# Two groups of value products moved to later steps of the masked slots in a six-layer attention kernel

## The reference, cut to what matters

```python
scores = jnp.einsum('bhqd,bhkd->bhqk', q, k) * scale
scores = scores * smask                       # (i & j) == 0
a = jax.nn.softmax(scores, axis=-1)
att = jnp.einsum('bhqk,bhkd->bhqd', a, v)
att = att.transpose(0, 2, 1, 3).reshape(Bx, Sx, Dx) @ wo + bo_
h = _ln(h + att, g1, be1)
ff = jax.nn.gelu(h @ w1 + b1_, approximate=False) @ w2 + b2_
h = _ln(h + ff, g2, be2)
```

## Time and profile before

| | us |
|---|---|
| median of 3 runs | 1603.87 (1602.07 to 1606.7) |
| the profiled execution, whole | 1600.91 |
| its span, first to last instruction | 1599.1 |
| PE busy | 1290.9 (81%) |
| DVE busy | 934.3 (58%) |
| ACT busy | 892.1 (56%) |
| POOL busy | 353.7 (22%) |

### The profile page before, as it was taken

One profiled execution on the slowest core, in us unless ns is written; L12 is line 12 of the kernel. 1 busy time (PEld: TensorE's weight loads), 2 busy tenths in 40 slices (PEclk: granted clock), 3 DMA queues, 4 the chain that ended last, 5 costly groups with the idle time before them and its releaser, 6 DMA issues.

```text
span 1599.1 us, 63841 instructions
## 1 busy us (share of the span) xinstructions
PE 1290.9 (81%) x28552; PEld 712.7 (45%) x28552; DVE 934.3 (58%) x1953; ACT 892.1 (56%) x1531; POOL 353.7 (22%) x567
## 2 busy tenths in 40 slices
PE   2678899889998989889998899888898887575833
PEld 1345555555555555455555555554343333131311
DVE  3554555555555556554555565545777577686456
ACT  1256666566666666666666666665455654243710
POOL 3122222222222222122222222132111010101021
PEclk7799999999999999999999999999999999798966
DMA  8443344423442443334433433342232221100000
GB/s 162 94 94 91 77 92 93 105 64 70 86 106 75 92 94 87 92 50 93 91 89 91 96 81 80 75 87 73 36 74 56 60 61 25 31 2 4 8 7 7
DMA packets 133895, 114.07 MB, mean 71 GB/s; under 512 B 42368, under 2 KB 121054, under 8 KB 133214
## 3 DMA queue, kind: packets, MB, share of 16 engines
q1 hardware_dynamic: 133622, 109.99, 31.4%
HBM read 62.69 MB, written 47.25 MB: 69 GB/s over the span
## 4 chain that ended last, share of the span: by engine, by line
PE 36%; issue 25%; DVE 22%; POOL 8%; ACT 5%; DMA 3%; SPq 1%; POOLq 0%; DVEq 0%; ACTq 0%
PE pD L711 14%; PE pT L711 7%; DVE MX L1105 7%; PE pV L781 7%; PE pS L728 5%; DVE DEN L1302 4%; PE pD L884 3%; DVE X L1227 2%; POOL RS L1421 2%; ACT PT L1013 2%; DVE R L1318 1%; DVE YE L1219 1%; ACT SQ L1028 1%; DVE CC L1157 1%; POOL VS L1481 1%
## 5 line engine op out<-in xcount | busy, mean ns | idle before, releaser
L1013 ACT ACTIVATE PT<-pT 128x512 f32<-128x512 f32 x1120 | 640.2, 596 | 506.4 <-PE pT L711 496.2
L1105 DVE TENSOR_REDUCE MX<-pS 128x1 f32<-128x512 f32 (+4 forms) x928 | 501.1, 574 | 440.5 <-PE pS L728 434.6
L711 PE MATMUL pT<-Qop,Kop 128*32 128x256 bf16 (+2 forms) x7168 | 454.3, 304 | 30.4 <-ACT PT L1013 20.9
L728 PE MATMUL pS<-Kop,Qop 128*32 128x128 bf16 (+4 forms) x7168 | 317.6, 259 | 86.9 <-DVE MX L1105 53.2
L781 PE MATMUL pV<-PT,Vp 128*32 128x256 f32 (+2 forms) x3584 | 319.8, 439 | 0.9 <-ACT PT L1013 0.7
L728 PEld LDWEIGHTS pS<-Kop,Qop 128*32 128x32 bf16 x7168 | 180.7, 98 | 266.2 <-DVE MX L1105 122.8
L711 PEld LDWEIGHTS pT<-Qop,Kop 128*32 128x32 bf16 x7168 | 186.9, 97 | 188.8 <-issue 87.1
L781 PEld LDWEIGHTS pV<-PT,Vp 128*32 128x32 f32 x3584 | 125.9, 111 | 69.6 <-issue 25.0
L1421 POOL TENSOR_TENSOR RS<-VAR,MHALF 128x4 f32<-128x4 f32 x60 | 60.6, 1011 | 419.4 <-DVE VAR L1164 419.4
L1455 POOL TENSOR_TENSOR ATT<-NUM,DEN 128x512 f32<-128x512 f32 x28 | 35.6, 1272 | 383.8 <-DVE DEN L1302 383.8
L711 PE MATMUL pD<-HIDT,W 128*32 128x512 f32 x768 | 105.5, 597 | 0.0
(11 more groups left out here) (146 smaller groups left out, 1284.2 us busy)
## 6 DMA issues: line engine op xcount, KB each, us to landing
Qop<-Qs SPq DMA_DIRECT2D x56, 384.0 KB
Kop<-Ks SPq DMA_DIRECT2D x56, 384.0 KB
Qs<-XS SPq DMA_DIRECT2D x28, 384.0 KB, 2.6
Ks<-XS SPq DMA_DIRECT2D x28, 384.0 KB, 3.0
Qs<-XS SPq DMA_DIRECT2D x28, 256.0 KB, 3.0
Ks<-XS SPq DMA_DIRECT2D x28, 256.0 KB, 3.0
EM<-Es SPq DMA_DIRECT2D x24, 256.0 KB, 3.2
Ms<-MROW SPq DMA_DIRECT2D x336, 4.0 KB, 1.4
```

The costliest lines, as they stand in the source:

```text
L711: ins = matmul(dst[c:min(c + 32, cols)], lhs[:, c:min(c + 32, cols)], rhs, start=start, stop=stop, tile_position=(0, c))
L728: ins = matmul(pS[32 * c:32 * c + 32, k % 2, at:at + w], Qop[:, it.par, h, R * qb:R * (qb + 1)], Kop[:, it.par, h, :] if qb == 0 or it.ful ...
L1013: ac.activation(dst, pT[:, k % 2, :], ACT.Exp, scale=SCALE).then_inc(t_used, 1)
L1105: ins = ve.tensor_reduce(MX[:, u, g2, qbs[0]:qbs[-1] + 1:step], pS[:, k % 2, at:at + w * len(qbs)].rearrange("p (h n) -> p h n", n=w), axi ...
```

## The change

The first step of group 0's value product in a slot with a masked C goes from 10 to 14, that of group 2 from 29 to 30. Group 1 (steps 23 to 25) and group 3 (0 to 2 of the next slot) stay.

```diff
                     if prev_last and step in ((1,) if Z.full else (0, 1, 2)):
                         value_product(Z, 3, [3] if Z.full else PIECES[step + 1])
-                    for g, first_step in ((0, 10), (1, 23), (2, 29)):
+                    for g, first_step in ((0, 14), (1, 23), (2, 30)):
                         if C is not None and not C.full and step - first_step + 1 in PIECES:
                             value_product(C, g, PIECES[step - first_step + 1])
```

## The result

The changed kernel takes 1625.91 us in the median of 3 runs (1621.4 to 1634.43) against 1603.87 us; the ratio is 1.0144, with a 95% interval of 1.0073 to 1.0214. A second comparison with more executions gave 1624.69 against 1607.2 us, ratio 1.0109 (1.0076 to 1.0142): 17.5 us slower, 12 to 23 us by the interval. Slower was forecast, with 13.2 us.

The account below looks back on a forecast made before the run. PE was taken to bound the kernel, busy 1290.9 of 1599.1 us. Terms 9.3 + 2.9 - 1.4 + 2.4 + 0 + 0 = +13.2 us on the 1603.87 us median gave 1617.1 us, range 1603 to 1628 us.

Parts of the forecast that it names:

- Sequence 0, the order: Group 0 falls behind the bias products' wait, of which 0.39 us is absorbed before VAR0: 6 x 1.55 = +9.3 us.
- Sequence 0, the clock: PE's half clock after the pause lengthened to 5.5 us: 6 x 0.4 = +2.4 us, ends 0 and 5.3.
- Sequences 2 and 3: Tiles 1 to 3 behind XC0 exceed the wait before VAR0, which starts 0.26 us later: 11 x 0.26 = +2.9 us.
- Sequence 1: Earlier R lets XC0 start about 0.7 us earlier, more work before VAR0: 5 x 0.27 = -1.4 us.
- Group 2: Steps 30 to 32: moved tiles just fit the gap before RB1, 0 us; ends 0 and 5.1 us in 23 slots.

Follow-up runs that it names:

- group 0 alone: Kernel before with only group 0's first step moved from 10 to 14, group 2 left at 29: ratio 1.0075, 12.1 us slower.
- group 0 with sequence 0 only: Kernel before with group 0 moved to step 14 only in the six slots whose Z is of sequence 0: ratio 1.0114, 18.3 us slower.
- group 2 alone: Kernel before with only group 2's first step moved from 29 to 30: ratio 1.0025, 4.0 us slower.
- group 0 elsewhere: Kernel before with group 0 moved to step 14 except where Z is of sequence 0: ratio 1.0023, 3.7 us slower.
- the filled pause: Changed kernel, score unit 13 repeated 18 times ahead of the bias products' wait in sequence-0 slots: ratio 1.0041, 6.6 us slower than before.
- the two fastest: Kernel before with sequence-0 bias products behind XC0: 0.9891; the same plus DVE's BQK ahead of DEN and its reciprocal: 0.9884, 1588.72 us.

## Why the prediction was right, and where it was not

- **Sequence 0, the order: right.** 1.55 us a slot was foreseen; the table has 48.42 - 46.96 = 1.46 and 48.47 - 46.86 = 1.61. The pause of 5.5 us, the lost wait before the variance and the place of the loss came as described, and the runs with group 0 in these slots only, and in all but these, put the whole loss there.
- **Sequence 0, the clock: mis-sized.** I had taken 0.4 us a slot, near the low end, since five of six rows showed the short stretch. It cost 0.8 to 1.1 us more, 5 to 7 us in six slots instead of 2.4, near the high end of my bound. The step that failed is the argument from counting. Five of the six rows were slots in which the clock fell with work already running, 0.7 to 1.4 us behind the pause; in the sixth, the long one, it fell inside the pause:

```profile
120.00:121.10 1.10, 0.00 (x0) 0.00 (x0) 0.96 (x2) 0.71 (x2) 1.10 (x2) 1.00 0.58 212
121.20:122.50 1.30, 0.00 (x0) 0.00 (x1) 0.75 (x1) 0.89 (x2) 1.04 (x1) 0.50 0.00 0
307.70:308.80 1.10, 1.10 (x76) 1.10 (x80) 0.11 (x1) 0.00 (x0) 0.00 (x0) 1.00 0.89 303
```

  In the traces with the pause of 5.5 us in the full kernel (after twice, group 0 alone, group 0 with sequence 0 only) the clock fell inside the pause in all 24 slots, and the work at the low level was 3.1 to 6.4 us long. With the pause of 3.76 us it was 3.2 to 3.4 us in 20 slots of 24 (before twice, group 2 alone, group 0 elsewhere) and 5.4 to 6.5 us in the other four. (A fall inside the pause does not suffice: three of the 20 short ones have it too, by 0.1 to 0.2 us.) So the longer pause makes the dear case common; the filled pause shows that it is the pause. But the size varies by trace: behind the same pause of 5.5 us the clock cost 0.3 to 1.7 us a slot more than before in these four traces.
- **Sequences 2 and 3: the number near, the mechanism wrong.** I had foreseen 0.26 us a slot between XC0 and the variance. None is there: the distance is 3.98 us with and without the change. I had reckoned PE's arrival from the end of the last matmul's row, which reaches past the time at which PE could have taken the next; that tail (583.10 + 0.39 = 583.49 against some 583.2) was free, and it just covers the 0.26 us. The table still has 0.1 to 0.25 us (sequence 2) and 0.4 us (sequence 3) more. Most of that comes from ahead of XC0. In the slots of sequence 2 without a stall there, RB1 to XC0 is 17.02 us in both kernels (17.10 once); with sequence 3 it is 17.02 us in most slots before and up to 17.9 us after, and I have no account of that. That the table's mean, 0.3 us, is near the 0.26 us foreseen is luck.
- **Sequence 1: right.** RB1 to XC0 fell from 18.29 us, the least before, to 17.47 us in two slots of five (17.9 to 18.0 us in most others), 0.3 to 0.8 us for the 0.7 foreseen, and XC0 to the variance grew from 3.70 to 3.94 us, 0.24 us for the 0.43 foreseen: the same free tail. Over whole slots the table shows a gain of 0.38 and 0.27 us, against the 0.27 us foreseen.
- **Group 2: right.** The variance to RB1 stays at 2.63 or 2.64 us in each of the 20 slots of the table, in both kernels. The idle time before the variance is 0.83 us, not about 1.
- **What no term held.** PE's waits without a releaser are 11.8 and 13.9 us in the two traces of before and 19.6 and 22.8 us in those of after, some 8 us more. That is as large as a term of the sum. The parts of the table, 6 x 1.53 + 6 x 0.95 - 5 x 0.33 + 5 x 0.18 + 5 x 0.43, make some 16 us; the spans of the traces differ by 20.5 us (first of each) and 25.9 us (second), and the stalls are what the table leaves out. The forecast's 13.2 us is below these 16 us by its clock term, some 3 us too small; its term for sequences 2 and 3 is right by number only, and it has none for the stalls.
- **Open:** what these stalls are. They are long in traces of slow and of fast variants alike (15.5 to 26.7 us in the ten others, 26.2 and 26.7 in the two fastest), so a long sum of them does not make a kernel slow by itself. But they are tied to places in PE's program, as the last section shows, so the edit may well have brought some; before had the fewest. No experiment was made on them.

## What to carry to other kernels

Look first for the longest wait of the engine that bounds the kernel, and keep independent work ahead of it in program order: moved behind it, 1.94 us of work lost all cover but the 0.39 us of one later wait. On TensorE a long wait can count twice: behind pauses of 3.76 to 5.5 us the matmuls ran at the low clock here. Better than choosing what stands ahead of the wait was to take the waiting instruction out of the way: the bias products behind XC0, which waits for less, made the kernel 17.5 us faster.

## What the runs showed of the hardware

Behind pauses of 4.6 and 5.5 us the stretch of work at 0.50 of the clock was 3.1 to 6.4 us long, behind 3.76 us it was 3.2 to 3.4 us (5.4 to 6.5 in four slots of 24), and behind 1.55 to 1.6 us there was mostly none (3.4 us once); behind waits of 1.95 us, in the run with both groups moved and the bias products late, it was 3.4 us in two slots of six. 24 us of superfluous matmuls that shortened the pauses made the kernel about 11 us faster.

The waits of PE without a releaser are single stalls, up to 2.7 us long. Two of them, at the same matmul inside a group of value products, in the first and in the second trace of after:

```profile
511.19 0.63 PE L781 MATMUL pV<-PT,Vp 128*32 128x512 f32 x3 [1.56 <-issue]
```

```profile
514.72 0.63 PE L781 MATMUL pV<-PT,Vp 128*32 128x512 f32 x3 [1.71 <-issue]
```

They keep to few places. I counted PE's matmuls in program order in the twelve traces of kernels with 28552 of them: the 317 stalls stand in front of only 58 different matmuls, though the order of the work differs between the kernels, and the distances between these 58 places are whole multiples of 126.7 matmuls, to within 2. So where PE can stall goes by the position in its program and not by the work that stands there; whether it does and how long differs from trace to trace. An edit that reorders work puts other work at these places. What happens there is not shown by any run.

The two microseconds ahead of the first of these stalls and the stall itself, as stretches:

```profile
507.60:509.60 2.00, 2.00 (x26) 0.62 (x17) 1.97 (x4) 1.32 (x3) 1.04 (x4) 1.00 0.66 95
509.60:511.20 1.60, 0.04 (x4) 0.01 (x2) 1.26 (x2) 1.59 (x2) 1.60 (x3) 1.00 0.00 0
```

Over the 23 stalls of 0.3 us or more in this trace the DMA share was 0.59 on average in the two microseconds ahead, against 0.37 over the stretch from 60 to 1240 us; in the other traces it was 0.44 to 0.63. That is a coincidence seen, not a cause shown.
